# Fused attention and gated MLP on eight cores: score work in units of 16 blocks and two full groups

## The reference

```
q, k, v = split(xn @ W_attn + b_attn), 16 heads of 64
att  = q @ k.T / sqrt(64) / temperature + slope[h] * (key position - query position)
w    = softmax(att over key <= query)
attn = (w @ v) @ W_proj + b_proj
ffn  = (silu(xn @ (w_gate/127).T) * (xn @ (w_up/127).T)) @ (w_down/127).T, hidden size 3072
```

## Time and profile before

| what | value |
|---|---|
| median of 3 runs | 948.58 us (947.56 to 952.15) |
| profiled execution | 950.44 us |
| its span, slowest core (4) | 948.9 us |
| spans of the eight cores | 941.3 to 948.9 us |
| TensorE, VectorE, ScalarE, GpSimd busy | 905.8, 497.7, 507.6, 296.5 us |
| score matmuls, first and last start | 100.0 and 676.1 us |
| mean granted TensorE clock, core 4 | 0.991 |

### The profile page before, as it was taken

How to read it: one execution, slowest core, us unless ns; L and a number is a source line. 1 busy time by engine, 2 the same in 40 slices (tenths; PEclk the granted TensorE clock), 3 DMA queues, 4 the chain that set the end, 5 groups by cost and what they waited for, 6 DMA issues and landing times.

```text
span 948.9 us, 18779 instructions; the slowest of 8 cores (941.3 to 948.9 us)
## 1 busy us (share of the span) xinstructions
PE 905.8 (95%) x6272; PEld 408.2 (43%) x6272; DVE 497.7 (52%) x1110; ACT 507.6 (53%) x605; POOL 296.5 (31%) x294
## 2 busy tenths in 40 slices
PE   3999999999999999999999999969989999999998
PEld 1444344444444444444444444423444444444443
DVE  4640577787777777777787777846521011110011
ACT  4754577777777776878777778646625200000000
POOL 1010233433433333433333333425553333321220
PEclk9999999999999999999999999979999999999999
DMA  8842279999999999999999999999998967351221
GB/s 269 263 136 88 47 142 214 197 210 234 202 200 210 194 204 220 209 198 213 191 195 223 203 190 198 191 206 210 240 292 273 304 228 266 128 208 59 89 89 44
DMA packets 333342, 182.16 MB, mean 192 GB/s; under 512 B 303680, under 2 KB 315968, under 8 KB 329664
## 3 DMA queue, kind: packets, MB, share of 16 engines
q1 hardware_dynamic: 327776, 164.13, 77.9%
q0 software_dynamic: 2304, 8.39, 2.7%
q10 hardware_dynamic: 3168, 8.44, 2.3%
HBM read 84.46 MB, written 20.97 MB: 111 GB/s over the span
## 4 chain that ended last, share of the span: by engine, by line
PE 71%; SPq 10%; DMA 7%; issue 6%; DVE 4%; ACT 2%; POOL 1%; DVEq 0%; ACTq 0%; POOLq 0%
PE ps_r L915 24%; PE ps_dn L1007 17%; PE ps_r L898 9%; SPq L396 7%; PE ps_s L967 6%; PE ps_dn L1014 6%; PE ps_y L982 4%; PE ps_r L938 4%; DMA xstage<-xin 2%; DMA h_sc<-hst 2%; DVE sc L676 2%; DMA stage_i<-wd_r 2%; ACT pr L830 1%; DVE st L622 1%; SPq L404 1%
## 5 line engine op out<-in xcount | busy, mean ns | idle before, releaser
L830 ACT ACTIVATE pr<-sc,cm 128x2048 bf16<-128x2048 f32 (+15 forms) x256 | 290.4, 1196 | 53.8 <-DVE cm L676 53.7
L676 DVE CUSTOM_DVE_ANT_0 sc<-ps_s,ramp 128x1024 f32<-128x1024 f32 (+7 forms) x256 | 243.7, 988 | 89.4 <-PE ps_s L967 82.6
L915 PE MATMUL ps_r<-xnT,wubuf 128*128 128x512 bf16 x768 | 207.8, 385 | 3.7 <-DVE hst L704 3.6
L915 PE MATMUL ps_r<-xnT,wgbuf 128*128 128x512 bf16 x768 | 206.9, 384 | 2.4 <-DVE hst L704 2.4
L1007 PE MATMUL ps_dn<-wdres,hb 128*128 128x512 bf16 x768 | 168.1, 380 | 0.0
L557 POOL TENSOR_SCALAR th_s<-th_s 128x512 f32<-128x512 f32 x96 | 59.2, 617 | 251.2 <-ACT th_s L751 251.2
L676 DVE CUSTOM_DVE_ANT_0 sc<-ps_s,ramp,cm 128x1024 f32<-128x1024 f32 (+7 forms) x128 | 99.9, 815 | 56.9 <-PE ps_s L967 56.9
L727 DVE SCALAR_TENSOR_TENSOR outsb<-ps_dn,xres 128x512 f32<-128x512 f32 x32 | 20.7, 687 | 200.3 <-PE ps_dn L1014 123.1
L898 PE MATMUL ps_r<-xnT,wqk_b 128*128 128x512 bf16 x512 | 120.9, 381 | 0.0
L563 POOL TENSOR_TENSOR gs_s<-th_s,gh_s 128x512 bf16<-128x512 f32 x96 | 111.3, 1159 | 28.7 <-POOL th_s L557 25.4
L1007 PEld LDWEIGHTS ps_dn<-wdres,hb 128*128 128x128 bf16 x768 | 75.0, 98 | 90.8 <-issue 0.4
(11 more groups left out here) (51 smaller groups left out, 529.2 us busy)
## 6 DMA issues: line engine op xcount, KB each, us to landing
stage_i<-wg_r SPq DMA_DIRECT2D x24, 512.0 KB, 5.4
stage_i<-wu_r SPq DMA_DIRECT2D x24, 512.0 KB, 6.3
h_sc<-hst SPq DMA_DIRECT2D x96, 128.0 KB, 2.9
hb<-h_sc SPq DMA_DIRECT2D x3, 3072.0 KB, 15.6
xstage<-xin SPq DMA_DIRECT2D x16, 512.0 KB, 7.1
stage_f<-wqk_r SPq DMA_DIRECT2D x8, 1024.0 KB, 7.0
xres<-xin POOLq DMA_DIRECT2D x16, 512.0 KB, 5.0
out<-outsb ACTq DMA_DIRECT2D x15, 512.0 KB, 2.7
```

The costliest lines, as they stand in the source:

```text
L676: e.tensor_tensor_reduce(scores(n, g + (2 if b == 2 else 0), c0, w), ps_s[:, g * 1024:g * 1024 + w], ramp[:, T - wide + c0:T - wide + c0 + ...
L830: e.activation(pr[n % 3][:, b0 * 128:(b0 + blocks) * 128], scores(n, r, 0, blocks * 128), AF.Exp, bias=cm[:, at:at + 1], scale=-1.0).then_ ...
L915: mm = e.matmul(ring(what, f), w[:, dc * 128:(dc + 1) * 128], xnT[:, dc * T + tb * 512:dc * T + tb * 512 + 512], start=(dc == 0), stop=(dc ...
```

## The change

Units now have 16 blocks. A head pair has 9: seven with the rows (14-j, j) for j from 0 to 6, one with row 15 alone and one with row 7 alone (8 blocks). A unit of 16 blocks has two steps and row 7 has one; each step is one full score group of 1024 columns of each head. The second group of a two-row unit holds the rest of the long row and the whole short row, as two *segments*, and VectorE makes a sum for each segment and head. Over the kernel this gives 72 units and 136 groups in place of 64 and 192.

ScalarE's order in a step changes. The long exponentials of a unit stand in its last step, between the tanh work of the gate products that end in the first half of the step and those of the second half. The short exponentials stand at the head of the next unit's first step, ahead of the evacuation of q or k. The two transposes of a unit move from its third step to the head of the next unit. `VY`'s transposition moves behind a later unit and no longer waits for the sums of the step that it stands in.

The `wqk` chunks after the first and the three early `wd` pieces are loaded and cast in halves, through `stage_f` and a new `stage_d`, in a list of their own (`EXTRAS`), each ordered when the one before it has been cast; the gate and up weights have `stage_i` to themselves. The first `wqk` chunk has its own `wq_f`. GpSimd's first casts no longer wait for `v_xn` and `a_cq`. `hst` has 5 buffers. Weight times V, the division, the planner and the block order in `VY` follow the new units; the tail's 9 steps of planner time 3000 become 6 of 4500.

```diff
-NU = 8 * NHP
+UNITS = [(14 - j, j) for j in range(7)] + [(15,), (7,)]
+NUP = len(UNITS)
+NU = NUP * NHP
 LAG = 3
+NHS = 5
...
+def batches_of(x):
+    rows = UNITS[x]
+    if rows == (15,):
+        return [[(0, 0, 1024)], [(0, 1024, 1024)]]
+    if rows == (7,):
+        return [[(0, 0, 1024)]]
+    i, j = rows
+    return [[(0, 0, 1024)], [(0, 1024, (i - 7) * 128), (1, 0, (j + 1) * 128)]]
+
+STEPS = [(n, b) for n in range(NU) for b in range(len(batches_of(n % NUP)))]
+NSB = len(STEPS)
+STEPS += [(n, b) for n in range(NU, NU + LAG) for b in range(2)]
...
 def rows_at(k):
...
+    rows = [(n, r) for r in range(2 * len(UNITS[n % NUP]))]
+    if b == 0 and not last_of(k):
+        return rows[:1]
+    return rows[1:] if b else rows
...
 def extra_loads():
+    items = {}
     for p in range(2, NHP):
-        f = FM[24 * (p - 2)] // 16 + 1 if p > 2 else 6
-        f = f + (2 - f) % 4
-        out[f] = ("q", p)
-    f = FM[24 * 7] // 16 + 1
-    f = f + (2 - f) % 4
+        f = FM[FIRST_OF[NUP * (p - 2)]] // 16 + 1
+        f += (1 - f) % 4
+        items[f], items[f + 2] = ("q", p, 0), ("q", p, 1)
+    f = FM[FIRST_OF[NUP * (NHP - 1)]] // 16 + 1
+    f += (1 - f) % 2
     for c in range(3):
-        out[f + 4 * c] = ("d", c)
+        items[f + 4 * c], items[f + 4 * c + 2] = ("d", c, 0), ("d", c, 1)
...
# SyncE
             def store_and_load(f):
                 store_h(f)
                 h, x = divmod(f, 4)
-                if x == 0 and f + 2 in EXTRA:
-                    load_staged(STAGED.index(EXTRA[f + 2]))
-                if (x == 0 and h and f + 2 not in EXTRA or f in EXTRA) and h + 2 < HCN:
-                    load_staged(STAGED.index(("g", h + 2)))
+                if x == 0 and 1 <= h and h + 2 < HCN:
+                    load_gu(h + 2)
+                if f in EXTRA and EXTRAS.index(EXTRA[f]) + 1 < len(EXTRAS):
+                    load_extra(EXTRAS.index(EXTRA[f]) + 1)
...
             for k in range(NST):
-                if k < NSB and k % 3 == 2:
-                    n = k // 3
-                    if n >= 3:
-                        e.wait_ge(sem["p_av"], n - 2)
+                n, b = STEPS[k]
+                if b == 0 and 1 <= n <= NU:
+                    if n > 3:
+                        e.wait_ge(sem["p_av"], n - 3)
                     for g in range(2):
-                        e.wait_ge(sem["a_e"], 4 * n + g + 3)
-                        turn(n, g)
+                        e.wait_ge(sem["a_e"], EXP_AT[n - 1, 2 * len(unit_of(n - 1)[2]) - 2 + g] + 1)
+                        turn(n - 1, g)
                 for f in ended(k, "u"):
                     store_and_load(f)
+                if b == 0 and n > LAG and (n - LAG) % NUP == 0:
+                    turn_y((n - LAG) // NUP - 1)
...
# VectorE
             def biased(k):
...
+                for seg, (at, c0, w) in enumerate(batches_of(x)[b]):
+                    for g in range(2):
+                        e.wait_ge(sem["p_s"], 2 * k + g + 1)
+                        if n:
+                            before = 2 * len(unit_of(n - 1)[2])
+                            e.wait_ge(sem["a_e"], EXP_AT[n - 1, g if b == 0 else before - 2 + g] + 1)
...
# ScalarE
             for k in range(NST):
-                if k < NSB and qk_at(k) is not None:
+                n, b = STEPS[k]
+                if b == 0 and 1 <= n <= NU:
+                    for r in range(2, 2 * len(unit_of(n - 1)[2])):
+                        weights(n - 1, r)
+                if qk_at(k) is not None:
                     evac_qk(*qk_at(k))
-                for f in ended(k, "g"):
+                for f in ended_half(k, "g", 0):
                     tanh_gate(f)
-                if k < NSB and k % 3:
+                if k < NSB and last_of(k):
                     for r in range(2):
-                        weights(k // 3, r + (0 if k % 3 == 1 else 2))
+                        weights(n, r)
+                for f in ended_half(k, "g", 1):
+                    tanh_gate(f)
...
# TensorE
             def score_batch(k):
...
+                for at, c0, w in batches_of(x)[b]:
+                    done = 0
+                    while done < w:
+                        wo = min(w - done, 512 - o % 512)
+                        for g in range(2):
+                            mm = e.matmul(ps_s[:, g * 1024 + o:g * 1024 + o + wo],
+                                          qst[p % 2][64 * g:64 * g + 64, rows[at] * 128:(rows[at] + 1) * 128],
+                                          kst[p % 2][64 * g:64 * g + 64, c0 + done:c0 + done + wo],
+                                          start=True, stop=True)
+                            if o + wo == 1024:
+                                mm.then_inc(sem["p_s"], 1)
+                        o += wo
+                        done += wo
```

More of the change, by code:

```diff
@@ new lines, in y_at, with y_block @@
+def y_at(x):
+    return sum(len(rows) for rows in UNITS[:x])
+def y_block(tt):
+    return [i for rows in UNITS for i in rows].index(tt)
+def batches_of(x):
[8 more added lines that the diff above has]
+NSB = len(STEPS)
@@ new lines, with last_of @@
+STEPS += [(n, b) for n in range(NU, NU + LAG) for b in range(2)]
+NST = len(STEPS)
+def last_of(k):
+    return k + 1 == NST or STEPS[k + 1][0] != STEPS[k][0]
+SUMS = [(k, seg, g) for k in range(NSB) for seg in range(len(batches_of(STEPS[k][0] % NUP)[STEPS[k][1]]))
+        for g in range(2)]
+SUM_AT = {what: o for o, what in enumerate(SUMS)}
+ROW_AT = {}
+for _k, _seg, _g in SUMS:
+    _n, _b = STEPS[_k]
+    ROW_AT[_n, 2 * batches_of(_n % NUP)[_b][_seg][0] + _g] = SUM_AT[_k, _seg, _g]
+EXPS = [(n, r) for n in range(NU) for r in range(2 * len(UNITS[n % NUP]))]
@@ L192, in ended, with ended_half @@
     return [GU[m // 8][1] for m in range(m0, FM[k]) if m % 8 == 7 and GU[m // 8][0] == what]
+def ended_half(k, what, half):
+    m0 = FM[k - 1] if k else 0
+    mid = m0 + (FM[k] - m0 + 1) // 2
+    a, b = (mid, FM[k]) if half else (m0, mid)
+    return [GU[m // 8][1] for m in range(a, b) if m % 8 == 7 and GU[m // 8][0] == what]
 def ended_late(what):
@@ L200, in extra_loads @@
 def extra_loads():
-    out = {}
+    items = {}
     for p in range(2, NHP):
-        f = FM[24 * (p - 2)] // 16 + 1 if p > 2 else 6
-        f = f + (2 - f) % 4
-        out[f] = ("q", p)
-    f = FM[24 * 7] // 16 + 1
-    f = f + (2 - f) % 4
+        f = FM[FIRST_OF[NUP * (p - 2)]] // 16 + 1
[3 more added lines that the diff above has]
+    f += (1 - f) % 2
     for c in range(3):
-        out[f + 4 * c] = ("d", c)
-    return out
+        items[f + 4 * c], items[f + 4 * c + 2] = ("d", c, 0), ("d", c, 1)
+    return items
 EXTRA = extra_loads()
[L218 to L241, removed]
+EXTRAS = [("q", 1, 0), ("q", 1, 1)] + [EXTRA[f] for f in sorted(EXTRA)]
+NEARLY = sum(1 for what in EXTRAS if what[0] == "d") // 2
 NLATE = HCP - NEARLY + 4
@@ L308, in build_program @@
         gh_s = [sb(st, f"gh_s{i}", [128, 512], BF16) for i in range(2)]
-        hst = [sb(st, f"hst{i}", [128, 512], BF16) for i in range(4)]
+        hst = [sb(st, f"hst{i}", [128, 512], BF16) for i in range(NHS)]
         VY = sb(st, "VY", [128, (NHP + 1) * VS], BF16)
@@ L368, in row @@
         def row(n, r):
[L371 to L374, removed]
+            p, _, rows = unit_of(n)
+            blocks = [i + 1 for i in rows]
+            return (rows[r // 2], 2 * p + r % 2, r % 2 * sum(blocks) + sum(blocks[:r // 2]), blocks[r // 2])
         def scores(n, r, c0, w):
-            long = 16 - unit_of(n)[2]
-            o = r % 2 * 17 * 128 + (long * 128 if r >= 2 else 0) + c0
+            o = r % 2 * 16 * 128 + ((unit_of(n)[2][0] + 1) * 128 if r >= 2 else 0) + c0
             return sc[:, o:o + w]
@@ L453, in _ @@
                 load_x(i)
-            e.wait_ge(sem["a_cq"], 1)
-            for o in range(4):
-                load_staged(o)
+            load_gu(0)
+            load_extra(0)
+            load_gu(1)
+            load_extra(1)
+            load_gu(2)
+            load_extra(2)
             def store_and_load(f):
```

286 lines of the change are left out of this document (133 added, 153 removed), and 4 rows, old and new, of the table SEMS.

## The result

The changed kernel takes 935.8 us (median of 4 runs) against 948.65: a ratio of 0.984, 95% interval 0.9818 to 0.9861. The forecast was 932, 918 to 952. The profiled execution took 936.4 us with a span of 934.8 on its slowest core, 7. Before, these were 950.4 and 948.9, so it is 14 us less. The mean of the eight spans went from 945.1 to 930.2, 15 us less.

What follows compares the result with a forecast made beforehand. The prediction took TensorE's own instructions and its stalls at the end of attention as the bound. Terms -11.5 + 3 + 1.5 - 9 = -16 took the profiled 950.4 to 934.4, 932.6 against the median, rounded to 932; range 918 to 952.

Steps and rivals of the forecast that it cites:

- Score groups: Attention stage, TensorE: 136 groups instead of 192, each costing about 0.205 us beside its columns, so 11.5 us less.
- ScalarE's order: Attention stage: long exponentials delayed by tanh work, 0.1 us in each of 32 units, 3 us more; bounds 0 and 35.
- the loop: Widest unit, scores through exponentials to next sums: 7.2 us, or 8.4 with a tanh ahead, against TensorE's 8.1.
- Rival C: ScalarE's loop becomes 9.2 us in 32 units as an evacuation also gets ahead: 35 us instead of 3, 964; chance 0.11.
- Transposes: SyncE's queue: 144 transposes instead of 128, taken as 0.2 us a head pair, 1.5 us more; ends 0 and 20.
- rival B: SyncE's queue becomes the bound, turns arrive late; sign: TensorE's `ps_y` waits for `pt`; 946 us, chance 0.10.
- The lead: Transposes landing ahead of first use: 9.6 us before, some 2 to 6 after, about nothing where `VY`'s transposition intervenes.
- The end: Last part of attention: TensorE's stalls and low clock, 18 us together, partly removed by the new loads: 9 us less.
- The low clock: Matmuls slowed behind the three end stalls: 1.9 us extra behind the first, an estimated 1.5 each behind the others.
- one wait of GpSimd of about 10 us: Last head pair: GpSimd waits for a late second-half `wd` load, costing 5 us of TensorE and 2 of clock.
- The cause I gave for the stall before: Attention's end: GpSimd sat 13.8 us before a `wd` cast, its load issued late behind transposes and running beside `VY`'s transposition.
- 56 handoffs fewer: TensorE to VectorE and back: fewer handoffs only save VectorE idle time, nothing on the path.

## Why the prediction was right

The sum was -16 us on the profiled execution and -14 was measured. The largest term, the score groups, was right in mechanism and size. That the rest came out near is in part luck: smaller terms missed in both directions. By its terms:

*Score groups, -11.5.* Right, and shown: putting 56 groups back cost 11.7 us by the medians, 11.1 in the attention stage. That no wait in the trace of before pointed at it was right too.

*ScalarE's order, +3.* Too high. TensorE's waits behind `cm` in the long stretch are 2.4 us against 2.1. But that the loop has no room was right: with the whole tanh work ahead of it, 27 us more. Rival C was a real danger, which the order in halves keeps away.

*Transposes, +1.5.* Too low: two waits for `pt`, 5.1 us, where there was none. This was to be the sign of rival B, and it came without B's time, so the sign was too blunt. The lead did shrink, unevenly. The transposes of the unit with row 15, whose lag holds the short unit, are these:

```profile
449.31 7.85 SPq L415 DMA_TRANSPOSE pt<-pr  x2
```

They end on the queue at 457.16, 2.1 us ahead of their first use at 459.22, where it was 11.9 before (328.90 to 340.75). For the unit behind the short one it is still 9.7 (465.64 to 475.35).

*The end, -9.* Its size was about right, in parts by luck. The waits fell from 13.0 to 8.5 us, 2.5 of which are for `pt`. The low clock behind them had been put at 5. Read from the starts it cost some 6 before: 2.6 behind the first stall, 1.7 behind the one that ends at 658.51, and 1.7 behind the last:

```profile
707.20 3.22 PE L915 MATMUL ps_r<-xnT,wgbuf 128*128 128x512 bf16 x8 [2.41 <-DVE hst L704]
710.22 2.29 PE L915 MATMUL ps_r<-xnT,wubuf 128*128 128x512 bf16 x8
712.34 1.89 PE L915 MATMUL ps_r<-xnT,wgbuf 128*128 128x512 bf16 x8
```

Sixteen matmuls take 5.1 us there where 3.4 would do. After the change it is 2.9, all behind the one stall of 3.27. So the end gave 4.5 + 3.1 = 7.6 of the 9. The forecast of one wait of GpSimd of about 10 us, 5 us of TensorE and 2 of clock was close: 11.5, 3.3 and 2.9.

The cause I gave for the stall before was incomplete. I put it on the `wd` load and on `VY` beside it; without the loads the kernel before won 5.3 us only, since the gate weights, with two f of lead behind the same transposes, then came late by themselves, with `VY` in the queue or without. So what helped was probably that the gate and up weights got a buffer and four f of lead of their own: GpSimd's 16.7 us of waits for them are gone, while those for `wd` grew from 19.6 to 31.6. No run tests that step alone.

*What was not in the sum.* TensorE's waits behind `hst` in the long stretch rose from 2.7 to 6.2 us. In VectorE's order four sums and the division now stand in one step ahead of the product that frees the bank. I had counted 56 handoffs fewer as nothing and did not ask what stands behind the longer run of sums in VectorE's order. The edit that moves the product takes half of these waits away; that the sums make the other half is not tested. And 2.0 us of waits between 100 and 150 us, which I had not looked at, are gone.

Together: groups -11.5; waits in the long stretch +6.4, at the end -4.5, at the start of the stage -2.0, so -0.1; low clock -3.1. That is -14.7 of the 15.9 that the attention stage lost on these two cores; 1.2 us stay open. The first stage was 1.8 us longer on these cores, for a reason that stays open, which leaves 14.1. The spans of the cores of one kernel differ by 8 to 9 us, so an agreement within 1 or 2 us should not be leaned on.

Two slips in the working changed nothing: the lower bound of the terms is -11.5 - 18 = -29.5 and not -32, and from GpSimd's cast at 627.23 to the product at 631.37 it is 4.1 us, not 3.6.

## What to carry to other kernels

Read the cost of a matmul from the distance of starts, by what stands ahead of it and behind: here a change between 64-row and 128-row matmuls cost 0.1 us each way as busy time, and no list of waits showed it; fewer and fuller groups gained just that. Where steps are merged, write down the loop through every engine that no longer has the merged step between, and what can get ahead in it; here half a step's tanh in the wrong place was worth 27 us. With SyncE's queue and the DMA engines as full as here, loads that were made earlier came with transposes that were later, so look at the sum of waits and not at the one that went away.

## What was not expected of the hardware

Moving eleven loads of `wqk` and six of `wd` (512 KB each) from SyncE's to GpSimd's queue took them out of SyncE's order, yet the transposes came later, 17.1 us of waits for `pt` (7.7 and 9.4 above) instead of 5.1. A typical transpose was as before, 2.5 us on the queue and 5.3 from issue to landing against 2.6 and 5.0; the longest were not, 10.5 and 15.4 us against 6.9 and 9.7. Whether the DMA engines were the limit, or the two queues shared them unevenly, no run here tells apart. And the time that a transpose holds the queue does not seem to be in proportion to the number of blocks alone, in the changed kernel:

```profile
L415 SPq DMA_TRANSPOSE pt<-pr x144: 1222/2640/6936, 112.8 to 673.4; - x144
```

The shortest, 1.22 us, stands against 1.93 for the shortest of 17 blocks; only the transposes of row 7 have 8 blocks, and half of 1.93 would be 0.97. This compares single shortest ones, so it is a hint and no more.
